# Attention block: first stores and loads issued from three queues, and the first twelve tiles' row maxima taken 1024 columns at a time

## The reference

```python
def _L0_attn_ref(x, Wq, bq, Wk, bk, Wv, bv, Wqv, bqv, Ws, bs, Wf, bf, Wr1, br1, Wr2, br2, g1, b1, g2, b2):
    ...
    xn = _ln(x, g1, b1)
    q = _lin(xn, Wq, bq).reshape(b, n, H, HD) / np.sqrt(HD).astype(np.float32)      # H = 16, HD = 8
    k = _lin(xn, Wk, bk).reshape(b, n, H, HD)
    score = jax.nn.softmax(jnp.einsum('bihd,bjhd->bhij', q, k), axis=-1)
    v = _lin(xn, Wv, bv).reshape(b, n, R, HD)                                       # R = 8
    out = jnp.einsum('bhij,bjrd->bihrd', score, v)
    qv = _lin(xn, Wqv, bqv).reshape(b, n, H, 1, QK) / np.sqrt(QK).astype(np.float32)
    qv = jnp.broadcast_to(qv, (b, n, H, R, QK))
    comp = jnp.concatenate([qv, out], axis=-1) @ Ws.T + bs
    comp = jax.nn.softmax(comp, axis=3)
    out = (comp * out).sum(axis=3).reshape(b, n, DIM)
    out = res + _lin(out, Wf, bf)
    res2 = out
    on = _ln(out, g2, b2)
    ffn = _lin(jax.nn.relu(_lin(on, Wr1, br1)), Wr2, br2)
    return res2 + ffn
...
x = L0_attn_x
x = x + _L0_attn_ref(_layernorm(x, axis=-1), ...)
x = x + _L0_ffn_ref(_layernorm(x, axis=-1), L0_ffn_W1, L0_ffn_b1, L0_ffn_W2, L0_ffn_b2)
```

## Time and profile before

| | us |
|---|---|
| median of 3 runs | 1235.48 (1234.93 to 1235.49) |
| the profiled execution, its own time | 1238.48 |
| span in the profile of that execution | 1236.7 |
| start of the first row scores (PE, line 990) | 41.45 |
| start of the first column scores (PE, line 1009) | 58.63 |

### The profile page before, as it was taken

The page is one execution under the profiler, slowest core; times in us unless marked ns, Lnnn a source line. Parts: engine busy times, 40 slices in busy tenths (PEclk is TensorE's granted clock), DMA queues, the critical chain, the costliest instruction groups (busy, mean ns, idle before and its releaser), DMA issues. The chain is left out here.

```text
span 1236.7 us, 27629 instructions
## 1 busy us (share of the span) xinstructions
PE 1175.7 (95%) x7997; PEld 541.9 (44%) x7997; DVE 961.8 (78%) x2115; ACT 758.4 (61%) x1463; POOL 956.9 (77%) x561
## 2 busy tenths in 40 slices
PE   4699999999999999999999999999999999977898
PEld 2134444444444444444444444444444444425675
DVE  7666788888888787878787888787888788786752
ACT  4056766666666666666667666666666666644443
POOL 5277888888889888889888888887978787863321
PEclk9599999999999999999999999999999999988999
DMA  5434444354544344444444453534444444320000
GB/s 127 126 73 102 104 104 110 86 118 94 117 104 115 89 108 100 104 96 110 111 96 108 103 112 88 121 92 104 104 104 104 104 104 105 69 52 1 18 25 26
DMA packets 60372, 115.52 MB, mean 93 GB/s; under 512 B 6656, under 2 KB 25568, under 8 KB 60336
## 3 DMA queue, kind: packets, MB, share of 16 engines
q0 software_dynamic: 18784, 67.70, 28.9%
q1 hardware_dynamic: 40770, 47.04, 11.7%
q10 hardware_dynamic: 782, 0.33, 0.1%
HBM read 22.51 MB, written 8.39 MB: 25 GB/s over the span
## 5 line engine op out<-in xcount | busy, mean ns | idle before, releaser
L1238 DVE TENSOR_REDUCE rowmax<-row_bank 128x1 f32<-128x512 f32 x1024 | 663.4, 686 | 187.2 <-PE row_bank L990 180.1
L1185 ACT ACTIVATE prob<-col_bank 128x512 f32<-128x512 f32 x1024 | 555.3, 594 | 283.4 <-PE col_bank L1009 281.7
L1019 PE MATMUL out_bank<-prob,v_op 128*64 128x512 f32 x2048 | 535.1, 594 | 0.2 <-ACT prob L1185 0.2
L1345 POOL TENSOR_TENSOR addend<-prob 128x1024 f32<-128x1024 f32 x128 | 317.5, 2481 | 48.4 <-ACT prob L1185 47.0
L1345 POOL TENSOR_TENSOR quad<-prob 128x1024 f32<-128x1024 f32 x128 | 334.6, 2614 | 18.5 <-ACT prob L1185 18.2
L990 PE MATMUL row_bank<-k_op,q_op 72*64 72x512 bf16 x2048 | 323.8, 386 | 12.1 <-DMA q_op<-q_parts 9.7
L1009 PE MATMUL col_bank<-q_op,k_op 74*64 74x512 bf16 x2048 | 318.4, 383 | 5.2 <-DMA q_op<-max_rows 3.7
L1009 PEld LDWEIGHTS col_bank<-q_op,k_op 74*64 74x64 bf16 x2048 | 117.3, 109 | 244.9 <-ACT prob L1185 205.5
L1019 PEld LDWEIGHTS out_bank<-prob,v_op 128*64 128x64 f32 x2048 | 154.0, 136 | 72.5 <-issue 11.7
L990 PEld LDWEIGHTS row_bank<-k_op,q_op 72*64 72x64 bf16 x2048 | 123.7, 109 | 139.0 <-DVE rowmax L1238 35.0
L1350 POOL DMA_DIRECT2D quad<-addend x128 | 112.6, 880 | 77.5 <-POOL addend L1345 72.9
(11 more groups left out here) (197 smaller groups left out, 809.7 us busy)
## 6 DMA issues: line engine op xcount, KB each, us to landing
quad<-addend POOLq DMA_DIRECT2D x128, 512.0 KB, 5.6
v_op<-v_all SPq DMA_DIRECT2D x64, 256.0 KB, 6.3
k_op<-k_parts SPq DMA_DIRECT2D x64, 144.0 KB
q_op<-q_parts SPq DMA_DIRECT2D x192, 48.0 KB
q_parts<-along_parts SPq DMA_DIRECT2D x11, 192.0 KB, 2.1
k_parts<-along_parts SPq DMA_DIRECT2D x33, 64.0 KB, 2.1
out<-y_out SPq DMA_DIRECT2D x8, 256.0 KB, 2.3
q_op<-max_rows SPq DMA_DIRECT2D x64, 4.0 KB
```

The source lines that it names most:

```text
L1019: last = nc.tensor.matmul(out_bank[ih * VW:(ih + 1) * VW, :], v_op[slot][:, t, :], halves(prob[:, t, :])[:, :, ih, :], start=(t == 0), sto ...
L1185: nc.scalar.activation(prob[:, t, h * HALF:(h + 1) * HALF], col_bank[h][:, :], ACT.Exp).then_inc(exp_done, 1)
L1238: nc.vector.tensor_reduce(rowmax[:, parity, t, h:h + 1], row_bank[h][:, :], AX.X, ALU.max).then_inc(max_done, 1)
L1345: pool.tensor_tensor(dst, prob[:, 2 * k, :], prob[:, 2 * k + 1, :], ALU.add).then_inc(pair_done, 1)
```

## The change

In `prepare`, a pair's four stores are divided anew: SP issues the queries and key part 0, POOL issues key parts 1 and 2. The four loads of unit 0's operands are issued by two engines: SP the keys and the first query part, ACT the other two query parts, both after the same waits as before. SP issues the stores of the last pair behind its two loads, no longer ahead of them. The values of unit 0 are loaded in the next block, behind the operands of unit 1.

In `attention`, the two row banks become one PSUM tensor of 1024 columns, and so do the two column banks. During the lead the tiles alternate between the two, and `wide_max` takes the maximum of 1024 columns in one instruction and raises `max_done` by two. The second column of `rowmax`, which these tiles don't write, is set to the lowest number ahead. `row_scores` gets the bank and the count to wait for as arguments. PE waits for all twelve maxima before group 0, since the column banks are used by it.

```diff
@@ -54,2 +54,3 @@
 EPS = 1e-5
+LOWEST = float(np.finfo(np.float32).min)
 LOADS = 1 + PARTS
@@ -109,8 +110,14 @@
     def load_scores(self, sp, u, slot):
+        self.load_keys(sp, u, slot)
+        self.load_queries(sp, u, slot, range(PARTS))
 
-        sp.dma_start(self.k_op[slot][0:PROD_ROWS, :], self.k_parts[ds(u, 1)].rearrange("u c d s -> u (c d) s")
-                     .to_broadcast([PARTS, PARTS * HD, SEQ])).then_inc(self.operands_in[slot], DMA)
-        for m in range(PARTS):
-            sp.dma_start(self.q_op[slot][m * PARTS * HD:(m + 1) * PARTS * HD, :],
-                         self.q_parts[m, ds(u, 1)].to_broadcast([PARTS, HD, SEQ])).then_inc(self.operands_in[slot], DMA)
+    def load_keys(self, queue, u, slot):
+        queue.dma_start(self.k_op[slot][0:PROD_ROWS, :], self.k_parts[ds(u, 1)].rearrange("u c d s -> u (c d) s")
+                        .to_broadcast([PARTS, PARTS * HD, SEQ])).then_inc(self.operands_in[slot], DMA)
+
+    def load_queries(self, queue, u, slot, parts):
+        for m in parts:
+            queue.dma_start(self.q_op[slot][m * PARTS * HD:(m + 1) * PARTS * HD, :],
+                            self.q_parts[m, ds(u, 1)].to_broadcast([PARTS, HD, SEQ])).then_inc(
+                self.operands_in[slot], DMA)
 
@@ -716,13 +723,13 @@
             load_x(2)
-            for n in range(PAIRS_BEFORE):
-                project.store(sp, n, n, True, [0, 1], project.stored if n < PAIRS_BEFORE - 1 else last_stored)
+            for n in range(PAIRS_BEFORE - 1):
+                project.store(sp, n, n, True, [0], project.stored)
             sp.wait_ge(ones_set, 1)
-            sp.wait_ge(project.stored, DMA * 3 * (PAIRS_BEFORE - 1))
-            sp.wait_ge(k_stored, DMA * (PAIRS_BEFORE - 1))
-            res.load_scores(sp, 0, 0)
-            sp.wait_ge(project.v_ready, TB // PAIR)
-            res.load_values(sp, 0, 0)
+            sp.wait_ge(project.stored, DMA * 2 * (PAIRS_BEFORE - 1))
+            sp.wait_ge(k_stored, DMA * 2 * (PAIRS_BEFORE - 1))
+            res.load_keys(sp, 0, 0)
+            res.load_queries(sp, 0, 0, [0])
+            project.store(sp, PAIRS_BEFORE - 1, PAIRS_BEFORE - 1, True, [0], last_stored)
             sp.wait_ge(x_in[2], DMA)
-            sp.wait_ge(last_stored, DMA * 3)
-            sp.wait_ge(last_k_stored, DMA)
+            sp.wait_ge(last_stored, DMA * 2)
+            sp.wait_ge(last_k_stored, DMA * 2)
 
@@ -756,3 +763,3 @@
             for n in range(PAIRS_BEFORE):
-                project.store(pool, n, n, False, [2], k_stored if n < PAIRS_BEFORE - 1 else last_k_stored)
+                project.store(pool, n, n, False, [1, 2], k_stored if n < PAIRS_BEFORE - 1 else last_k_stored)
             pool.wait_ge(rows_in, DMA * len(rows))
@@ -784,2 +791,5 @@
                                  ACT.Copy).then_inc(wf_copied, 1)
+            act.wait_ge(project.stored, DMA * 2 * (PAIRS_BEFORE - 1))
+            act.wait_ge(k_stored, DMA * 2 * (PAIRS_BEFORE - 1))
+            res.load_queries(act, 0, 0, [1, 2])
 
@@ -917,4 +927,5 @@
 
-        col_bank = [pb(f"col_bank{n}", [P, HALF]) for n in range(2)]
-        row_bank = [pb(f"row_bank{n}", [P, HALF]) for n in range(2)]
+        col_pair, row_pair = pb("col_bank", [P, 2 * HALF]), pb("row_bank", [P, 2 * HALF])
+        col_bank = [col_pair[:, n * HALF:(n + 1) * HALF] for n in range(2)]
+        row_bank = [row_pair[:, n * HALF:(n + 1) * HALF] for n in range(2)]
         out_bank = pb("out_bank", [P, HALF])
@@ -970,4 +981,6 @@
 
-            for u in (1, 2):
-                res.load(sp, u, 0, u)
+            res.load_scores(sp, 1, 1)
+            for u in (0, 1):
+                res.load_values(sp, 0, u)
+            res.load(sp, 2, 0, 2)
             ffw.load(sp, a)
@@ -983,9 +996,9 @@
         def _(pe):
-            def row_scores(v, slot, t, known_free):
+            def row_scores(v, slot, t, bank, free):
 
                 for h in range(2):
-                    if not known_free:
-                        pe.wait_ge(max_done, 2 * TB * v + 2 * t + h - 1)
+                    if free is not None:
+                        pe.wait_ge(max_done, free + h)
                     for c in range(2):
-                        last = nc.tensor.matmul(row_bank[h][c * VW:(c + 1) * VW, :],
+                        last = nc.tensor.matmul(bank[h][c * VW:(c + 1) * VW, :],
                                                 q_op[slot][0:PROD_ROWS, t * P + c * VW:t * P + (c + 1) * VW],
@@ -1064,3 +1077,3 @@
                                 pe.wait_ge(operands_in[sv], LOADS * DMA * (Gv + 1))
-                            row_scores(u - s + av, sv, tv, False)
+                            row_scores(u - s + av, sv, tv, row_bank, 2 * TB * (u - s + av) + 2 * tv - 1)
                         if t > 0:
@@ -1124,6 +1137,6 @@
             for t in range(TB):
-                row_scores(0, 0, t, t == 0)
+                row_scores(0, 0, t, (row_bank, col_bank)[t % 2], 2 * t - 2 if t > 1 else None)
             pe.wait_ge(operands_in[1], LOADS * DMA)
             for t in range(LEAD - TB):
-                row_scores(1, 1, t, False)
+                row_scores(1, 1, t, (row_bank, col_bank)[t % 2], 2 * TB + 2 * t - 2)
                 if t == 0:
@@ -1133,2 +1146,3 @@
             pe.wait_ge(onehot_set, 2)
+            pe.wait_ge(max_done, 2 * LEAD)
             group(0, True, False, True)
@@ -1240,2 +1254,8 @@
 
+            def wide_max(v, parity, t):
+
+                dve.wait_ge(row_scored, 2 * TB * v + 2 * t + 2)
+                nc.vector.tensor_reduce(rowmax[:, parity, t, 0:1], (row_pair, col_pair)[t % 2][:, :], AX.X,
+                                        ALU.max).then_inc(max_done, 2)
+
             def split_max(w, parity, step):
@@ -1311,2 +1331,3 @@
             dve.memset(max_parts[:, :, :], 0.0)
+            dve.memset(rowmax[:, :, :, :], LOWEST)
             dve.memset(onehot[:, :, :], 0.0).then_inc(onehot_set, 1)
@@ -1316,5 +1337,5 @@
             last.then_inc(onehot_set, 1)
+            dve.wait_ge(onehot_set, 2)
             for t in range(TB):
-                for h in range(2):
-                    row_max(0, 0, t, h)
+                wide_max(0, 0, t)
             for step in range(3):
@@ -1322,4 +1343,3 @@
             for t in range(LEAD - TB):
-                for h in range(2):
-                    row_max(1, 1, t, h)
+                wide_max(1, 1, t)
             group(0, True, False, True)
```

## The result

The changed kernel takes 1244.52 us, the median of 6 runs (1242.7 to 1244.93); the kernel before, run beside it, 1235.49 (1234.49 to 1237.39). The ratio is 1.0063, with a 95% interval of 1.0051 to 1.0074: 0.6% slower, which on 1235.49 is 7.8 us, between 6.3 and 9.1. The profiled execution took 1244.37, with a span of 1242.6.

What follows compares the result with a forecast made beforehand. PE, busy 95% of the span, was taken to bound the kernel, so only group 0's start mattered. A later start of row scores (+0.7 us) and longer lead (+5.8) gave 1235.48 + 6.5 = 1242.0 us, range 1239.2 to 1244.6.

## What to carry to other kernels

When a producer raises a semaphore by two at once, check every waiting count for the odd values: a wait for an odd count is a wait for the next even one, and can undo a double buffer (7.2 us of the lead here). A block's end waits for the last transfer of its list, so what is issued last should not be a store behind long loads: put a store that the barrier needs ahead of loads that crowd a few DMA engines. And read the DMA share of a wait in engines: 0.19 is three of sixteen, and a new order of rows, at little cost here (the query stores of the units land after 2.5 us instead of 2.1), took more out of the kernel than any reordering of work around these loads.

## What the hardware showed

Three things I had not expected. Reductions of 512 columns in a row start 0.60 us apart while each takes 0.68 to 0.69, so two of them take 1.20 in a row. Wide ones of 1.22 us start 1.14 apart where their banks are free, so widening could save 0.06 a tile at most, and in this lead the banks' refill took more than that (1.23 a tile). A 4 KB transfer came up to 0.8 us too late in 8 of 63 units behind loads of 288 KB on three engines, and kept PE waiting in none when these loads ran on more. And the same program issued its first loads at 34.47 in one execution and at 36.69 in the other, and ended within 0.5 us of the same span.
